# Exps of the cross attention in halves of two banks, with a warm-up exp and new places in the lead-in, in a fused decoder layer

## The reference

```
x: (32,128,128)  ctx: (32,77,128)
# linear attention
q = gelu(x Wq^T + bq) + 0.21 ; k = gelu(x Wk^T + bk) + 0.21 ; v = x Wv^T + bv
z = 1 / (q . mean(k) + 1e-6)                     # by head
kv = (rope(k)^T v) / n ; out = rope(q) kv * z
x = layernorm(x + (norm(out + x) * gamma + beta))
# cross attention, 16 heads of 8
scores = Q K^T / sqrt(8) ; attn = softmax(scores) ; x = layernorm(x + (attn V) Wo + bo)
# experts
probs = softmax(x router_w + router_b) ; the 4 largest, scaled to sum 1 -> c
y = sum over e of c[e] * (gelu(x w1[e] + b1[e]) w2[e] + b2[e])
x = layernorm(x + y)
```

## Time and profile before

| | us |
|---|---|
| median of 3 runs | 627.86 |
| lowest, highest | 626.38, 630.57 |
| profiled execution | 629.56 |
| its span | 627.1 |
| TensorE busy in it | 593.1 (95%) |
| VectorE busy | 418.9 (67%) |
| ScalarE busy | 406.3 (65%) |
| POOL busy | 242.9 (39%) |

### The profile page before, as it was taken

One profiled execution on the slowest core, in us unless ns is written; L12 is line 12 of the kernel. 1 busy time (PEld: TensorE's weight loads), 2 busy tenths in 40 slices (PEclk: granted clock), 3 DMA queues, 4 the chain that ended last, 5 costly groups with the idle time before them and its releaser, 6 DMA issues. The chain is left out here.

```text
span 627.1 us, 16585 instructions
## 1 busy us (share of the span) xinstructions
PE 593.1 (95%) x6513; PEld 434.3 (69%) x6513; DVE 418.9 (67%) x1472; ACT 406.3 (65%) x519; POOL 242.9 (39%) x166
## 2 busy tenths in 40 slices
PE   7898979999999999999999999999999998999994
PEld 3644735787677876877677867786777866676664
DVE  2457377666777778678868677678767775365445
ACT  2337536885559765885669655975678657965651
POOL 5336413443344426163434334342525342234342
PEclk9897698999999999999999999999999999999998
DMA  7622020010200120011100210012000110000000
GB/s 175 190 77 70 26 61 14 20 29 11 60 22 2 46 70 19 4 46 40 50 3 2 63 54 19 4 45 71 19 3 19 29 44 4 19 1 2 1 18 18
DMA packets 31541, 23.05 MB, mean 37 GB/s; under 512 B 2744, under 2 KB 30152, under 8 KB 31464
## 3 DMA queue, kind: packets, MB, share of 16 engines
q1 hardware_dynamic: 23801, 16.59, 9.0%
q10 hardware_dynamic: 7311, 4.97, 2.7%
q0 software_dynamic: 352, 0.43, 0.5%
HBM read 13.90 MB, written 5.46 MB: 31 GB/s over the span
## 5 line engine op out<-in xcount | busy, mean ns | idle before, releaser
L717 ACT ACTIVATE g<-ps,b 128x512 f32<-128x512 f32 x256 | 168.1, 685 | 86.3 <-PE ps L1004 85.1
L536 POOL TENSOR_TENSOR gl<-g,gh 128x1024 f16<-128x1024 f32 x64 | 138.3, 2160 | 212.3 <-ACT gh L706 212.3
L1363 DVE SCALAR_TENSOR_TENSOR acc<-ps,cw,acc 128x128 f32<-128x128 f32 x448 | 125.4, 342 | 103.0 <-PE ps L1027 57.3
L1027 PEld LDWEIGHTS ps<-w,g 128*128 128x128 f32 x1024 | 121.6, 192 | 9.8 <-issue 4.6
L1027 PE MATMUL ps<-w,g 128*128 128x128 f32 x1024 | 127.0, 277 | 0.2
L1002 PE MATMUL ps<-x2h,w1h 128*128 128x512 f16 x256 | 98.0, 383 | 8.9 <-ACT g L717 8.1
L1003 PE MATMUL ps<-x2l,w1h 128*128 128x512 f16 x256 | 97.7, 382 | 0.0
L1004 PE MATMUL ps<-x2h,w1l 128*128 128x512 f16 x256 | 97.5, 381 | 0.0
L1023 PE MATMUL ps<-w2h,gh 128*128 128x128 f16 x512 | 89.2, 219 | 1.7 <-DVE acc L1363 1.5
L1025 PE MATMUL ps<-w2h,gl 128*128 128x128 f16 x512 | 89.0, 219 | 0.0
L1024 PE MATMUL ps<-w2l,gh 128*128 128x128 f16 x512 | 89.0, 219 | 0.0
(11 more groups left out here) (188 smaller groups left out, 869.3 us busy)
## 6 DMA issues: line engine op xcount, KB each, us to landing
q_rep<-q_parts SPq DMA_DIRECT2D x24, 128.0 KB
x<-in_x SPq DMA_DIRECT2D x8, 256.0 KB, 3.2
w_stage<-in_L_ffn_w ACTq DMA_DIRECT2D x1, 2048.0 KB, 13.2
q_swap<-q SPq DMA_DIRECT2D x16, 128.0 KB, 2.1
q_parts<-qx SPq DMA_DIRECT2D x16, 128.0 KB, 1.7
k_rep<-k_parts SPq DMA_DIRECT2D x24, 77.0 KB
out<-fin SPq DMA_DIRECT2D x7, 256.0 KB, 2.5
k_parts<-kx SPq DMA_DIRECT2D x8, 154.0 KB, 2.1
```

Source lines behind the costliest of these rows:

```text
L536: pool.tensor_tensor(gl[:, j % SPLIT_RING, :, :], g32[:, e % RING, :, :], gh[:, j % SPLIT_RING, :, :], ALU.subtract).then_inc(s["lo"], 1)
L717: act.activation(g32[:, e % RING, h, :], bH[:, h, :], ACT.Gelu, bias=b1[:, e, h:h + 1], scale=1.0 / WS).then_inc(s["gelu"], 1)
L1027: m = pe.matmul(o, g32[:, e % RING, h, tok], w2[:, j, h, :], start=(h == 0), stop=(h == HALF - 1))
L1363: m = dve.scalar_tensor_tensor(out=(acc_all if e == E - 1 else acc)[:, b, :], in0=second_bank(f, e)[:, b * P:(b + 1) * P], scalar=cw[:, b, ...
```

## The change

In every group, the exp of a sequence becomes two, each over two banks (77x1024), and scores_t is split into two halves of 8 matmuls, each with its own wait for the exp half that read its banks and its own count of t_p. All counts of t_p and prob in other waits are doubled. ScalarE's wait for t_p now stands inside the loop over halves, behind those for av_p and i_wl. In group 0 a small exp of 128x1 stands ahead of the first one. All tables of the lead-in (..._FIRST, ..._EARLY, ..._ONE, the fillers and the weights' places) have new numbers; the tables of the steady bodies and the ..._ZERO tables are the same.

```diff
-PE_FIRST = dict(x_t=4, q=4, kv01=9, cx_t=6, kv23=26, v1=13, k=32, k_mean=36, kv=43, den=46, out=49, x1_t=51,
+PE_FIRST = dict(x_t=0, q=3, kv01=3, cx_t=5, kv23=11, v1=21, k=45, k_mean=14, kv=40, den=43, out=44, x1_t=51,
...
-HIGH_W = (28, 67, 73, 77, 77, 85)
+HIGH_W = (71, 84, 89, 93, 96, 125)
...
+        warm_exp = sb("warm_exp", [P, 1])
...
-                since(sp, "t_p", B * a)
+                since(sp, "t_p", 2 * B * a)
...
                     if p == at["scores_t"][b]:
-                        since(act, "t_p", n + 1)
-
+                        if n == 0:
+                            act.activation(warm_exp[:, :], xbq[:, :], ACT.Exp)
                         since(act, "av_p", n - 1)
                         act.wait_ge(s["i_wl"], 4)
-                        act.activation(prob[:, b % 2, :].rearrange("p (r n) -> p r n", r=4), ps[0:CTX, 0:4, :],
-                                       ACT.Exp, scale=float(HD) ** -0.5).then_inc(s["prob"], 1)
+                        for half in range(2):
+                            two = slice(2 * half, 2 * half + 2)
+                            since(act, "t_p", 2 * n + half + 1)
+                            act.activation(prob[:, b % 2, :].rearrange("p (r n) -> p r n", r=4)[:, two, :], ps[0:CTX, two, :],
+                                           ACT.Exp, scale=float(HD) ** -0.5).then_inc(s["prob"], 1)
...
-                since(pe, "prob", n)
-                for i in range(BLK):
-                    for r in range(4):
-                        m = pe.matmul(ps[0:CTX, r, i * P:(i + 1) * P], k_rep[32 * r:32 * r + 32, i, b * CTX:(b + 1) * CTX],
-                                      q_rep[32 * r:32 * r + 32, i, b * P:(b + 1) * P], start=True, stop=True)
-                m.then_inc(s["t_p"], 1)
+                for half in range(2):
+                    since(pe, "prob", 2 * (n - 1) + half + 1)
+                    for i in range(BLK):
+                        for r in (2 * half, 2 * half + 1):
+                            m = pe.matmul(ps[0:CTX, r, i * P:(i + 1) * P], k_rep[32 * r:32 * r + 32, i, b * CTX:(b + 1) * CTX],
+                                          q_rep[32 * r:32 * r + 32, i, b * P:(b + 1) * P], start=True, stop=True)
+                    m.then_inc(s["t_p"], 1)
...
-                since(pe, "prob", n + 1)
+                since(pe, "prob", 2 * (n + 1))
```

More of the change, by code:

```diff
@@ L93 @@
 POOL_AT = dict(x_beta=19, k_rot=25, q_rot=20, res=28, norm1=34, norm2=46, x1=11, x2=61, finish=37, low=2)
-PE_FIRST = dict(x_t=4, q=4, kv01=9, cx_t=6, kv23=26, v1=13, k=32, k_mean=36, kv=43, den=46, out=49, x1_t=51,
[L96 to L100, removed]
+PE_FIRST = dict(x_t=0, q=3, kv01=3, cx_t=5, kv23=11, v1=21, k=45, k_mean=14, kv=40, den=43, out=44, x1_t=51,
+                q_x=63)
+PE_EARLY = dict(scores=(0, 0, 0, 0, 0, 0, 0, 0), max_t=6, scores_t=(11, 19, 27, 33), values=(21, 31, 41, 43),
+                u_t=(49, 49), ao_t=51, wo=52, x2_t=59)
+PE_ONE = dict(x_t=0, q=0, kv01=0, kv23=0, k_mean=11, kv=16, den=31, out=35, cx_t=44, v1=45, k=50, x1_t=55,
+              q_x=56)
 PE_ZERO = dict(x_t=0, q=10, kv01=15, kv23=17, k_mean=23, kv=27, den=29, out=31, cx_t=39, v1=50, x1_t=59, k=57,
@@ L104 @@
                ao_t=49)
-ACT_FIRST = dict(x_t=6, q=8, cx_t=14, kv23=16, k=21, x1_t=47, q_x=63)
-ACT_EARLY = dict(max_t=21, scores_t=(23, 28, 30, 37), u=(34, 42), ao_t=44, x2_t=57)
-ACT_ONE = dict(x_t=0, q=5, kv23=20, cx_t=44, k=45, x1_t=47, q_x=51)
+ACT_FIRST = dict(x_t=0, q=0, cx_t=23, kv23=7, k=47, x1_t=51, q_x=60)
+ACT_EARLY = dict(max_t=30, scores_t=(39, 40, 44, 50), u=(50, 53), ao_t=56, x2_t=63)
+ACT_ONE = dict(x_t=1, q=8, kv23=26, cx_t=55, k=57, x1_t=60, q_x=60)
 ACT_ZERO = dict(x_t=3, q=11, kv23=20, cx_t=48, x1_t=62, k=55, q_x=63, max_t=22, scores_t=(29, 30, 35, 37),
                 x2_t=63, weights=0, c_t=53, gelu=3, high=3, u=(36, 45), ao_t=52)
[L110 to L114, removed]
+DVE_FIRST = dict(q=9, kv01=7, kv23=14, v1=16, k_rot=14, k_mean=15, q_sin=15, k=49, kv=19, den=42, out=47,
+                 norm1=48, norm2=52, x1=56, q_x=56, xl=6)
+DVE_EARLY = dict(scores=(0, 0, 0, 0, 0, 0, 3, 3), max=4, pairs=(32, 40), wo=57, x2=62, x2_t=63)
+DVE_ONE = dict(q=8, kv01=0, kv23=1, k_rot=16, k_mean=20, q_sin=25, kv=23, den=31, out=31, norm1=31, v1=33,
+               norm2=44, k=45, x1=56, q_x=63, xl=0)
 DVE_ZERO = dict(q=20, kv01=14, kv23=16, k_rot=21, k_mean=23, kv=28, den=29, out=31, norm1=33, norm2=35, x1=46,
@@ L118 @@
                 cw_hl=25)
-POOL_FIRST = dict(x_beta=25, k_rot=4, q_rot=13, res=29, norm1=50, norm2=53)
-POOL_EARLY = dict(x1=6, x2=63)
-POOL_ONE = dict(x_beta=11, k_rot=34, q_rot=35, res=57, norm1=61, norm2=63)
+POOL_FIRST = dict(x_beta=48, k_rot=2, q_rot=19, res=24, norm1=50, norm2=55)
+POOL_EARLY = dict(x1=48, x2=63)
+POOL_ONE = dict(x_beta=30, k_rot=26, q_rot=30, res=30, norm1=33, norm2=62)
 POOL_ZERO = dict(x_beta=22, k_rot=20, q_rot=20, res=27, norm1=27, norm2=42, x1=11, x2=52, finish=6, low=2)
 FILL_START = 17
-PE_FILL0 = dict(q=2, kv01=12, kv23=0, k_mean=0, kv=0, den=0, out=2, v1=0, k=10, x1_t=50, q_x=1)
-PE_FILL1 = dict(q=8, kv01=5, kv23=0, scores=0, max_t=1, scores_t=4, kv=11, den=0, out=0, k_mean=7, values=0,
-                wo=3, q_x=1, x2_t=0, v1=0, x1_t=15, u_t=43)
-HIGH_W = (28, 67, 73, 77, 77, 85)
[L130 to L134, removed]
+PE_FILL0 = dict(q=1, kv01=12, kv23=5, k_mean=11, kv=1, den=1, out=0, v1=0, k=16, x1_t=25, q_x=1)
+PE_FILL1 = dict(q=8, kv01=4, kv23=0, scores=0, max_t=7, scores_t=9, kv=0, den=0, out=0, k_mean=0, values=37,
+                wo=5, q_x=3, x2_t=9, v1=3, x1_t=7, u_t=57)
+HIGH_W = (71, 84, 89, 93, 96, 125)
+LOW_W = (69, 69, 80, 88, 90, 127)
+SCALE_W = (41, 86)
+LOAD_W = (2, 2, 31, 73)
+W1_W = (24,)
+ROWS_W = (4, 31)
 def build(nc, A, consts, where, out):
@@ L838, in entry @@
                     pe.wait_ge(s["ld_cx"], 16 * (a + 1))
-                    since(pe, "prob", B * a)
+                    since(pe, "prob", 2 * B * a)
                     for b in range(B):
@@ L888, in cross @@
                         since(pe, "u", 2 * g + pair + 1)
-                        since(pe, "prob", B * (g + 1))
+                        since(pe, "prob", 2 * B * (g + 1))
                         for n in range(4):
```

## The result

| | before | after |
|---|---|---|
| median of 21 runs each, side by side | 628.81 us | 630.64 us |
| lowest, highest | 625.75, 630.57 | 626.51, 636.79 |
| span of the profiled execution | 627.1 | 628.8 |

The change made the kernel slower: the ratio of the times is 1.0044, 95% interval 1.0027 to 1.0061, so about 2.8 us. (The medians are 1.8 us apart; the times after spread further upward.) That lies within the 1% that the forecast called "within". The median is 1.0 us above the stated 629.6; as a move it is 1.8 to 2.8 us against the 1.7 that was forecast.

What follows compares the result with a forecast made beforehand. TensorE's queue bounds from about 91 us, with ScalarE without slack in cross attention; before that, chains through all engines. Lead-in -2.1 (-2.6 - 1.5 + 2.0) and +3.9 behind it give +1.8: 629.6 us, range 623.0 to 635.0.

Steps and rivals of the forecast that it cites:

- within: Whole kernel: time stays within 1% (6.3 us) of before, chance 0.76, against faster 0.11 and slower 0.13.
- Steady groups: Groups 1 to 7: split exps and a later table load add 3.9 us, from +1.5 to +6.
- The split: ScalarE, each steady exp: two halves cost 0.10 us more than one whole, 0.40 a group, before small idle-time gains.
- The table load's wait: Exp's table load on ScalarE also waits for t_p: 0.25 us later in groups 2 to 6, 1.05 in group 7.
- Body 0: Cross attention of group 1: load not early, two short ScalarE waits removed, counted as 0.
- Lead-in, first body: Start to x1 transposes: earlier kv01, fillers at a faster clock, less waiting; -2.6 us, from -1.0 to -3.4.
- Lead-in, second body: x1 transposes to end of values: group 0 exps without gaps, TensorE clock limiting; -1.5 us, between 0 and -4.
- From values to the first expert matmul: Lead-in's end: work ahead of u transposes and a later y2, less the q_x pair; +2.0 us, +1 to +3.
- y2 behind x1: VectorE late in the lead-in: y2 now stands behind a POOL rstd and x1 of group 1, +2.1 us.
- A: Each scores_t: halves cost TensorE too, +5 to +7 us on top, 636 us; chance 0.13.
- C: TensorE slack absorbs halves and table delay, and lead-in gains and losses cancel: 627.9 us; chance 0.20.
- B: Lead-in gets the full clock, -6.4 us there, halves nearly free at +1.5: 623 us; chance 0.22.

Runs made afterwards that it cites:

- the places alone: Code of the kernel before, with whole exps, and the change's new lead-in tables, against the kernel before: 627.64 us, ratio 0.9985.
- the best version: The change with halves in group 0 only and the last weight load at place 32, against the kernel before: 623.63 us, ratio 0.9931; again 622.41 us, 0.9905.

## Why the prediction was right, and where it was not

The total was right, 629.6 against 630.64, but in part by luck: the second body of the lead-in came out 3.8 us worse than forecast, and body 0, the first body, the steady groups and the last stretch of the lead-in together 3.8 us better. The measured terms below are from one profile each.

- **Steady groups, forecast +3.9, measured +3.3** (2.57 + 0.71). The mechanism is as forecast: a split that ScalarE passes on, and a table load that inherits the wait for t_p. The sizes inside it were off. The split was put at 0.30 us a group, net of 0.10 of small gains; it is 0.13. A pair lasts 1.93 us, not 2.00: I took the nearest row, a cast, and a half exp is 30 ns shorter. A pair costs 0.06 more than a whole exp and not 0.10, so four cost 0.24, and less the 0.10 that is about what was measured. The table load's wait was put at 0.25 and is 0.42 (0.36 of it stands in the row at 187.31). In the last group the wait was put at 1.05 and cost 0.56, by the kernel with the old order of waits.
- **Body 0, forecast 0, measured -1.4.** The prediction had no term for it. The earlier trace rows show the full clock from 160 us on, and I let that regime begin at 91. It does not. In body 0 of the kernel before, from 94 to 98 us:

```profile
84.00:88.00 4.00, 3.34 (x15) 1.43 (x14) 2.71 (x13) 0.59 (x1) 1.07 (x1) 1.00 0.28 62
94.00:98.00 4.00, 3.72 (x25) 1.30 (x26) 2.52 (x8) 3.12 (x6) 0.00 (x0) 0.57 0.16 55
```

  and in after (columns as in the earlier trace rows):

```profile
84.00:88.00 4.00, 3.97 (x18) 1.55 (x16) 2.71 (x15) 2.36 (x4) 1.01 (x1) 1.00 0.30 63
94.00:98.00 4.00, 3.85 (x39) 1.62 (x39) 3.50 (x9) 3.97 (x8) 0.50 (x1) 1.00 0.02 6
```

  TensorE waits some 2.1 us for the first gelu in both. Behind that wait the granted clock was 0.57 before and 1.00 after, and ahead of it TensorE was busy 3.34 of 4 us before and 3.97 after. Body 0 was 67.5 to 67.7 us in eight of the nine profiles with the new places, and 69.0 to 69.5 in the four with the old places and in the one of the places alone. The fuller stretch does not explain it. At the same distances from its first expert matmul, the kernel of the places alone shows 3.97 of 4 us ahead of the wait and a clock of 0.58 behind it, and the one with x1 behind y2 a clock of 0.64 ahead and 1.00 behind. The places alone were profiled in their longest execution of twelve, so its body 0 may be longer than usual. What keeps the clock stays open.
- **Lead-in, first body, forecast -2.6, measured -3.3.** As worked out: kv01 3.25 us sooner (13.50 instead of 16.75) at the full clock, and output matmuls in 1.26 us instead of 1.92. Over all profiles the x1 transposes stand at 35.2 to 37.9 with the new places and at 39.7 to 40.2 with the old ones.
- **Lead-in, second body, forecast -1.5, measured +2.3** (x1 transposes to the end of values: 34.9 us, now 37.2). This is the step that failed. It said "ScalarE's loads and weight scalings moved here have over 10 us until their readers", and put no other cost on them. The load's own reader has that time; what it meets on the DMA engines has not. Its place number hardly changed (74 to 73), but only one high part stands ahead of it in that body where there were two (HIGH_W has 71, and had 67 and 73), and it is issued at 42.90, among the loads of q_rep, instead of at 47.85, behind them. The scores began 4.2 us behind the issue of q_rep's last load instead of 2.0. Moving that one load takes 1.75 us off, as shown above. It does not settle the rest. With the load early the stretch took 33.1 to 33.2 us in three profiles, 1.7 less than before, near the -1.5 forecast, and 37.4 in two; with the load late it took 36.6 to 37.3 in four. In the ratios the move is worth 0.56% (some 3.5 us) with halves everywhere, 0.5 to 0.8% with halves in group 0 and 0.3% with whole exps.

  Beyond the 1.75 us the nine profiles with the new places differ in what ran at half clock. Two things vary: the nine fillers ahead of the first scores_t take 2.10 us or 3.4 to 4.0, and the values of the second sequence, 32 matmuls, take 1.1 to 1.5 us or 1.94. In the three short stretches neither is slow, in the two of 37.4 us both are, and in the four with the load late just one of the two is. One kernel is among the short ones in one execution and among the long ones in another, so the load's place alone does not decide it. What does is open.
- **From values to the first expert matmul, forecast +2.0, measured +0.9.** Two of its terms came as forecast. y2 behind x1 cost 2.3 us (7.23 us behind the values before, 9.54 now) where 2.1 was put, and from x2n's end to the first expert matmul it is 2.54 us instead of 3.85, 1.3 less where 1.4 was put. The +1.3 for cx, fillers and v1 ahead of the u transposes did not come: the matmuls with Wo, which y2 needs, end 7.4 us behind the values where they ended 7.2 behind them. And y2 waits for x1 until later than that, so a delay ahead of Wo and one ahead of x1 run beside each other and do not add up. And x1 ahead of y2 is no loss on the whole: undone in the best version, it cost 2.5 us, since TensorE's queue takes x1 first.
- **Rivals.** A: refuted, 0.02 us each. C: its first half is refuted by the steady bodies; its second, that the lead-in's gains and losses cancel, is what the profile shows (first th 0.13 us sooner). B came in part: the full clock at the start, some of it in the values (2.46 us instead of 3.70 for 64), and body 0. Without collision and steady halves the kernel takes 622.4 to 623.6 us, which is where B's 623 was put, but B kept the steady halves, at +1.5.

## What to carry to other kernels

When a wait moves behind another in front of an instruction for which the compiler adds its own, ask which of them the added one takes: here it took the two written last in both orders, and the place of one line cost 0.42 us a group. A load moved to a free place of its queue is to be laid against every small transfer in flight at that time, not against its own reader. Where a split pays only at one place (here the exps of group 0), make it only there: with the load moved, halves everywhere had a ratio of 0.9988, whole exps 0.9956, and halves in group 0 alone 0.9905 to 0.9931. With the load late, halves in group 0 gave nothing (0.9982 against 0.9985), so one such change can hide what another is worth. And where one kernel's lead-in differs between executions, as here by 4 us in one stretch, take two profiles of it before explaining such a difference between two kernels.

## What the runs showed of the hardware that was not expected

- With a load of 512 KB issued among three loads of 128 KB, the time from the end of the last small one's issue to its use went from 2.0 to 4.2 us, at a DMA share of 0.90.
- A TensorE wait of 2.1 us was followed by 3.5 us at half clock in five profiles and by none in eight, after nearly the same work. With the same exps, body 0 took 69.05 us in the one case and 67.49 in the other (places alone, load late and early).
- One kernel ran the same nine fillers in 4.00 us in one execution and in 2.10 in another.
